# A decoder layer on one core: a third bank for cross scores, the second tile's query projection moved ahead of value and key groups, and query groups and latents spread over the end of a stage

## What is computed

```python
x = x + attn(layernorm(x))      # q,k,v projections, rope, masked softmax, out @ wo.T
x = x + xattn(layernorm(x), ctx)
#   qp = q @ Wq.T ; k, v = split(ctx @ Wkv_expand.T)
#   softmax(causal(qh @ kh.T / 4)) @ vh @ Wout.T
h = silu(z @ w_gate) * (z @ w_up)   # z = layernorm(x)
x = x + sparsify_2to4(h) @ w_down
```

## Time and profile before

| | us |
|---|---|
| median of 3 runs (442.87 to 443.71) | 443.65 |
| the profiled execution, its own time | 448.27 |
| span of the profiled execution | 446.5 |
| PE busy | 394.7 |
| DVE busy | 286.2 |
| ACT busy | 202.2 |
| POOL busy | 159.9 |

### The profile page before, as it was taken

The page is one execution under the profiler, slowest core; times in us unless marked ns, Lnnn a source line. Parts: engine busy times, 40 slices in busy tenths (PEclk is TensorE's granted clock), DMA queues, the critical chain, the costliest instruction groups (busy, mean ns, idle before and its releaser), DMA issues.

```text
span 446.5 us, 7877 instructions
## 1 busy us (share of the span) xinstructions
PE 394.7 (88%) x2912; PEld 320.3 (72%) x2912; DVE 286.2 (64%) x616; ACT 202.2 (45%) x524; POOL 159.9 (36%) x159
## 2 busy tenths in 40 slices
PE   4988899889899999869899999979899999577794
PEld 3767777667698777747698877857698877345783
DVE  3696931788769932748769961578769931344273
ACT  1422641477334741557444552287344551386230
POOL 4358730378310420356520340267520430155000
PEclk9996999999999999989999999999999999869698
DMA  7976300240001400240000510232000500210000
GB/s 239 373 253 206 95 25 23 73 119 19 2 0 54 143 23 25 72 124 12 2 1 7 166 25 1 70 112 51 0 1 0 167 24 24 84 36 1 1 0 23
DMA packets 34292, 29.93 MB, mean 67 GB/s; under 512 B 18512, under 2 KB 28880, under 8 KB 34000
## 3 DMA queue, kind: packets, MB, share of 16 engines
q1 hardware_dynamic: 34256, 29.44, 21.1%
HBM read 20.26 MB, written 5.24 MB: 57 GB/s over the span
## 4 chain that ended last, share of the span: by engine, by line
PE 64%; DVE 14%; DMA 7%; issue 5%; ACT 4%; SPq 3%; POOL 2%; POOLq 0%; DVEq 0%; ACTq 0%
PE ps L526 13%; PE ps L587 10%; PE ps L404 9%; PE ps L472 6%; PE ps L601 6%; DVE rope L728 4%; PE ps L435 4%; PE ps L512 3%; DMA q<-qx 3%; PE ps L490 3%; PE ps L412 2%; DMA prob<-in_masks 2%; POOL prob L934 2%; DVE total L759 2%; DVE mx L745 2%
## 5 line engine op out<-in xcount | busy, mean ns | idle before, releaser
L934 POOL TENSOR_TENSOR prob<-prob,inv 128x512 f32<-128x512 f32 x80 | 83.0, 1042 | 105.9 <-DVE inv L765 105.7
L404 PE MATMUL ps<-xnT,wqk_sb 128*128 128x256 f32 x320 | 79.1, 397 | 1.0 <-ACT xnT L989 0.7
L404 PEld LDWEIGHTS ps<-xnT,wqk_sb 128*128 128x128 f32 x320 | 61.5, 198 | 13.9 <-issue 4.9
L1026 ACT ACTIVATE prob<-ps,mx 128x128 f32<-128x128 f32 (+1 forms) x128 | 52.7, 431 | 13.7 <-DVE mx L743 11.6
L1036 ACT ACTIVATE pT<-ps 128x512 f32<-128x512 f32 x80 | 47.8, 601 | 18.6 <-PE ps L472 18.4
L728 DVE TENSOR_TENSOR rope<-ps,trig_sb 64x512 f32<-64x512 f32 x80 | 55.0, 688 | 1.1
L927 POOL TENSOR_TENSOR qs<-rope 128x512 f32<-128x512 f32 x32 | 40.9, 1278 | 37.6 <-DVE rope L728 37.6
L472 PE MATMUL ps<-ident_sb,prob 128*128 128x128 f32 x320 | 49.9, 281 | 4.5 <-POOL prob L934 4.2
L472 PEld LDWEIGHTS ps<-ident_sb,prob 128*128 128x128 f32 x320 | 37.7, 142 | 12.5 <-POOL prob L934 8.4
L743 DVE TENSOR_REDUCE mx<-ps 128x2 f32<-128x512 f32 (+1 forms) x48 | 33.1, 690 | 20.1 <-PE ps L454 19.7
L913 POOL TENSOR_TENSOR rstd<-vareps,power 128x1 f32<-128x1 f32 x24 | 13.1, 550 | 88.5 <-DVE vareps L707 88.3
(11 more groups left out here) (86 smaller groups left out, 677.7 us busy)
## 6 DMA issues: line engine op xcount, KB each, us to landing
k<-kx SPq DMA_DIRECT2D x32, 128.0 KB, 2.9
q<-qx SPq DMA_DIRECT2D x32, 128.0 KB, 2.6
vb<-v_sb SPq DMA_DIRECT2D x56, 64.0 KB, 2.1
wqk_sb<-in_wqk SPq DMA_DIRECT2D x4, 512.0 KB, 8.2
work<-in_wgu SPq DMA_DIRECT2D x4, 512.0 KB, 9.4
wo_sb<-in_wo SPq DMA_DIRECT2D x1, 2048.0 KB, 15.8
x_ln<-in_x SPq DMA_DIRECT2D x4, 256.0 KB, 2.8
x_res<-in_x SPq DMA_DIRECT2D x4, 256.0 KB, 3.0
```

Source lines behind the costliest of these rows:

```text
L404: mm = pe.matmul(o[:, half, :], wqk_sb[:, k, g, half, :], xnT[:, 0, k, :], start=(k == 0), stop=(k == KT - 1))
L934: pool.tensor_tensor(p, p, inv[:, i % ND, 0:g].unsqueeze(2).broadcast_to([P, g, 512 // g]), ALU.mult).then_inc(s_norm, 1)
L1026: ins = act.activation(prob[:, i % ND, h * k:(h + 1) * k], ps[:, BANK_S + i % 2, h * k:(h + 1) * k], ACT.Exp, bias=mx[:, i % ND, h:h + 1], ...
```

## The change

- **Third bank for cross scores.** `scores_bank(i)` gives units of the cross stage one of three banks: the two old ones and the bank of ring slot 2. Cross scores then wait for the exp three units back. The third unit waits for the drain of `xq1`, the last user of the slot. In return the query groups of the cross stage use slots 0 and 1 in turn, and the latent values, the next user of slot 2, wait for all exps.
- **Bridge.** The tile-0 norm comes after two pairs instead of one, value tile 0 moves from ahead of the pairs to behind them, and tile 1's norm and query projection stand inside and behind key group 0, ahead of value tile 1 and key group 1. DVE makes the low part of tile 1's queries before the rope of key group 1, ACT copies each value tile behind that tile's queries, and ACT's copy of key group 1 moves behind the second cross exp.
- **End of the stage.** `X_FILL` places q5 at 13 and q6 at 15 (before: q5 at 12, q6 behind the loop). `latent_kv` becomes two functions: values ahead of the last out projection, keys behind the `ln3` transposes. On ACT the latent values are copied ahead of `x3_hi`; the copy of the keys stays where it was.
- SP's queue keeps its order; the context load waits for the latent keys instead of the latent values. In the prologue latent values come before latent keys.

```diff
-X_FILL = {1: 0, 3: 1, 5: 2, 7: 3, 9: 4, 12: 5}
+X_FILL = {1: 0, 3: 1, 5: 2, 7: 3, 9: 4, 13: 5, 15: 6}
...
-USES = [("wo0", 0), ("ln1", 1), ("v0", 1), ("wo1", 0), ("ln20", 2), ("xq0", 1), ("v1", 2), ("k0", 1), ("ln21", 0),
+USES = [("wo0", 0), ("ln1", 1), ("wo1", 0), ("ln20", 2), ("xq0", 1), ("v0", 2), ("k0", 1), ("ln21", 0), ("xq1", 2),
...
+def scores_bank(i):
+    return BANK_S + i % 2 if i < NQB else (BANK_S, BANK_S + 1, BANKS_M[2])[(i - NQB) % 3]
...
             def unit_scores(b, i):
...
+                if b and i < 2:
+                    pe.wait_ge(s_exp, u - 2)
+                elif 2 <= i < NQB + 2:
+                    pe.wait_ge(s_sub, NQB * b + i - 1)
+                elif i == NQB + 2:
+                    wait_drained(pe, "xq1", b)
+                elif i > NQB + 2:
+                    pe.wait_ge(s_exp, u - 2)
+                o = ps[:, scores_bank(i), :]
...
+            def latent_values(b, n):
                 pe.wait_ge(s_ctx, 16 * n)
+                claim("xv", b)
+                if b is not None:
+                    pe.wait_ge(s_exp, UNITS * (b + 1))
...
+            def latent_keys(b):
                 claim("xk", b)
...
+                window_out(b, 1, pair=0)
+                window_out(b, 1, pair=1)
+                cross_norm(b, 0, n)
+                window_out(b, 1, pair=2)
+                cross_q(b, 0)
+                window_out(b, 1, pair=3)
                 if more:
                     wait_drained(pe, "ln1", b)
                     v_tile("v0", b, 0)
...
+                    rope_group("k0", b, QG, halves=(0,))
+                cross_norm(b, 1, n)
+                if more:
+                    rope_group("k0", b, QG, halves=(1,))
+                cross_q(b, 1)
                 if more:
                     v_tile("v1", b, 1)
...
+                if more:
+                    latent_values(b, b + 2)
                 cross_out(b, 1)
                 if more:
-                    rope_group("q6", b, 6)
                     rope_group("q7", b, 7)
                 transpose_norm("ln3", b, 3 * b + (4 if more else 3))
+                if more:
+                    latent_keys(b)
...
                 if more:
                     unit_scores(b + 1, 0)
-                    latent_kv(b, b + 2)
                 down(b, 0)
```

More of the change, by code:

```diff
@@ L530, in window_out @@
                     mm.then_inc(filled(use, b), 1)
-            def latent_kv(b, n):
+            def latent_values(b, n):
                 pe.wait_ge(s_ctx, 16 * n)
+                claim("xv", b)
+                if b is not None:
+                    pe.wait_ge(s_exp, UNITS * (b + 1))
+                for t in range(TT):
+                    mm = pe.matmul(half_banks("xv", b)[:, t, :], ctx_sb[:, t * P:(t + 1) * P], xwv_sb[:],
+                                   start=True, stop=True)
+                mm.then_inc(filled("xv", b), 1)
+            def latent_keys(b):
                 claim("xk", b)
@@ L540, in latent_kv @@
                 mm.then_inc(filled("xk", b), 1)
-                claim("xv", b)
-                for t in range(TT):
-                    mm = pe.matmul(half_banks("xv", b)[:, t, :], ctx_sb[:, t * P:(t + 1) * P], xwv_sb[:],
-                                   start=True, stop=True)
-                mm.then_inc(filled("xv", b), 1)
             def cross_norm(b, t, n):
@@ L967, in batch @@
                 if more:
-                    next_group(b, "q6", 9)
                     next_group(b, "q7", 10)
@@ L1108, in batch @@
                         unit_exp(b, NQB + i)
-                    if i == 0 and more:
+                    if i == 1 and more:
                         keys(1, RG * (b + 1) + 2)
@@ L1113, in batch @@
                 cross_outputs(b, 1)
+                if more:
+                    latent_values(b)
                 wait_filled(act, "ln3", b)
```

57 lines of the change are left out of this document (19 added, 38 removed).

## The result

The changed kernel takes **456.4 us** (median of 4 executions, 453.83 to 457.91) where the kernel before takes 443.3 beside it (441.71 to 443.71): a ratio of **1.0265**, 95% interval 1.021 to 1.0321. The forecast was 449.0 and its range ended at 454.0; the loss is more than twice the one forecast, and in the direction forecast. The profiled execution took 457.18 us, with a span of 455.4.

What follows compares the result with a forecast made beforehand. DVE bounds gate to T5 (unit 5's window transposes), PE and the softmax chain T5 to gate. Front 0.7 plus end 1.0 is 1.7 us per batch, 5.1 in three; 443.65 + 5.1 = 448.8, said as 449.0, range 444.0 to 454.0.

Steps and rivals of the forecast that it cites:

- S2's and S4's waits: Cross scores of units 2 and 4: PE's waits for exp (1.44 us) and DMA (1.05), batch 0, go.
- T9: Transposes of unit 9, end of cross stage: now ahead of q5, so PE waits 1.1 us for POOL.
- first pair: First window pair of the bridge: a wait of 0.8 us for ACT's last window output in batches 0 to 2.
- second `ln3`: Second `ln3` transposes, behind the out projection: PE waits 0.6 us, as q7 alone covers DVE and POOL's 3.59.
- The first max: First cross max on DVE, behind key group 1's rope: starts 2.3 us behind the first cross score.
- Gate to T5: First gate matmul to unit 5's transposes, next window stage: bound by DVE, stays 35.3 us, gain 0.
- Batch 1's late transfer: Cross-stage DMA wait in batch 1: 4.3 us in the profiled execution, taken as absent from ordinary executions.
- the first rival: PE's clock falls in the new wait ahead of units 0 and 1's transposes: 454.1 us, 18 in 100.
- T0's and T1's waits: Transposes of cross units 0 and 1: PE waits about 0.7 and 2.3 us for POOL.
- End of the stage: End of cross stage: +1.9 us to the out projection, -1.0 from there to the gate, +0.9 to +1.0 per batch.
- Front: Front of a batch, up to unit 1's transposes: +0.7 us per batch, their start 94.15 instead of 93.47.
- Batch 3: 0: Last batch, without filler: third bank only lengthens the wait for the same DMA; 0, between -0.3 and +0.3 us.

Runs made afterwards that it cites:

- e2_latents_back: e1_two_banks with latent keys and values put back where they stood before, behind the first scores of the next window stage: 449.70 us.
- e4_third_clean: The kernel before with the third score bank alone, query group 6 in the bank that the scores have left: 448.75 us.
- e1_fill_wait: The changed kernel with two extra matmuls that compute nothing ahead of unit 1's transposes in batches 0 to 2: 452.48 us.
- e1_two_banks: The changed kernel with cross scores in two banks instead of three, everything else as changed: 451.29 us.
- e2_end_alone: The kernel before with only the end of the cross stage and the latents as in the change, bridge and two banks as before: 448.73 us.
- e4_bridge_clean: The changed kernel with end of stage and latents put back as before, query group 6 in the bank that the scores have left: 452.76 us.
- e2_half_q6: The kernel before with query group 6 issued in two halves, the first ahead of the last pair of cross values: 443.23 us.
- e3_v1_inside: The kernel before with value tile 1 moved behind the second cross score and half of key group 1 in its place, two banks: 439.83 us.
- e1_max_first: The changed kernel with the first cross max ahead of key group 1's rope on DVE: 452.91 us.

## Why the prediction was wrong, point by point

**Right.** The direction. Which waits go and which come: S2's and S4's waits gone in batches 0 to 2, T0 0.5, T1 2.2, T9 1.1, first pair 0.8, second `ln3` 0.5 us, all as forecast within 0.2 us. The first max comes 2.3 us behind S0 (85.30, 87.63). Gate to T5 is 35.36, and e2_latents_back shows it to be the same with the latents in it: the FFN stage gains nothing. Batch 1's late transfer was in one of the two traced executions of before. The third bank gives no gain in schedule (e4_third_clean, batch 2; e1_fill_wait beside e1_two_banks).

**Failed: the clock was left out of the sum.** The sum had nothing for it; the first rival had 18 in 100, and "the waits are split by one unit's work" was the reason against it. T0's and T1's waits are split by 1.0 us of work (91.25 to 94.47 - 2.22); that didn't hold the clock. What did hold it in the traced executions was a piece of work that takes the place of most of the wait (e1_fill_wait), or a bank wait that leaves the idle time in two shorter pieces further apart (e1_two_banks: S2's wait ends at 89.43, S4's begins at 92.67). The price forecast for it, 1.7 us a batch, was about right for the changed kernel: 104.0 and 103.9 against 102.5 is 1.5 and 1.4. Between the medians it is 456.4 - 452.5 = **3.9 us**. How this is shared out over the batches of an ordinary execution was not traced; the 1.9 us by which the two profiles differ in batch 3 (93.95 and 92.08) can't be counted as the filler's or the change's, as batch 3 has no filler and varies as much between kernels with the same batch 3. The trace of before had shown the price in its one long wait. The range was drawn to hold this rival but ended at 454.0, with the rival itself at 454.1; the rival alone would not have reached 456.4 either.

**Failed: two terms too small.** Per batch 1.7 us were forecast and 2.7 measured with the clock held, 8.1 to 8.5 in all. *End of the stage*: +1.0 forecast, +1.55 measured (e2_end_alone). The piece from q5's old place to the out projection grew by 2.2 instead of 1.9, and the piece from there to the gate shrank by 0.8 instead of 1.0. In the changed kernel the second `ln3` transposes come 3.59 us behind the out projection (118.67 to 122.26), as forecast, but from them to the gate it takes 1.43 us (to 123.69) instead of 1.16: the latent keys, which start at 122.63, take 1.06 us instead of 0.96 and don't fit, so that they, and no longer the wait for `x3_hi`, set the gate. The latent values take 1.05 (117.62 to 118.67). Of the 0.15 us that are left, 0.1 is the gate's wait for `x3_hi` in batch 0 of before, which is longer than in the others (0.78 and 0.69). *Front*: +0.7 forecast, about 1.1 measured. T1 is 0.3 later than forecast, since S0 is (85.30, forecast 85.0); and from T1 to T9's earliest start it takes 15.83 us (94.47 to 111.40 - 1.10) where before it was 15.53 (93.47 to 109.00). "From T1 on PE is the bound again (group, scores, transposes, values in the same order as before)" was 0.3 us short. Most of it, 0.2, stands at T3: from its scores to its values it takes 1.03 us (98.50 to 99.53), before 0.84 (97.46 to 98.30); what T3 waits for was not tested.

**Sum with what was measured.** 443.3 + 3 x 2.7 + 3.9 = 455.3 against 456.4. The 3.9 is a difference of medians itself, so what this tests is the 8.1: e1_fill_wait is 8.5 above before in its own series. The 1.1 left over is no more than the medians of before differ between series (443.2 to 445.8).

**"Batch 3: 0"** was not contradicted: 92.08 to 92.21 with three banks (e1_fill_wait, e4_bridge_clean, e4_third_clean), 92.06 and 92.78 before, each with a granted clock of 0.90 to 0.94 over the batch. In the changed kernel's profile it was 93.95 at 0.88, and 94.21 at 0.88 in e2_half_q6. Differences of 2 us or less in this batch can't be told from the clock.

**Open.** Why the clock falls behind a wait in one batch and not in the next of the same execution, and what share batch 3 has in the 456.4.

## What to carry to other kernels

A buffer added ahead of a chain that has another limit turns several short waits into one long one; the idle time was the same here, but TensorE came out of it at half clock in some batches. Before adding a buffer, ask what is late next, and whether its wait will stand in one piece. Better than a buffer was independent work in the wait, taken from a place ahead of the chain: that shortens what stands before the chain too (e3_v1_inside). Work should leave the stretch in which its engine is the bound, not enter it. And if a new wait like the 1.8 to 2.9 us here stands in the forecast's own sum, the clock's price belongs in the sum, weighted, and not among the rivals.

## What the runs showed of the hardware

- **The same wait costs differently from batch to batch.** In e4_third_clean PE ran at 0.50 behind a wait of 2.92 us (batch 0), and at 1.00 behind one of 2.83 us (batch 2), with the same instructions around them. In the changed kernel, after 0.5 and 2.2 us, the clock held in batch 0 and fell in batches 1 and 2. In e1_max_first, after a single wait of 1.79 us, it held in batch 1 and fell in batches 0 and 2. The windows behind both waits of e4_third_clean are shown above.
- **The spread of the times shrank with the filler.** The changed kernel's executions lie between 453.83 and 457.91, and those of the kernel with the wait filled between 452.06 and 452.71. A wide spread is no sign of such a wait, though: 21 executions of before lie between 440.61 and 446.48.
- **The clock is low in batch 3 of every traced execution.** Over this batch, which has no filler, the granted clock is 0.88 to 0.94, also in the kernel before (0.94 and 0.90).
- **One transfer can be late once**: S4's wait of 3.55 us in one batch of one execution, 0.95 in the same place of another, and behind it PE's granted clock was 0.72 for six us.
